# Splitting a W2 tile over TensorE's column groups by feature instead of by rank, and turning it on VectorE

## The chip, the cores and the metric

The kernel runs on one core of one Trainium2 chip. The metric is the time of one execution on the device, in microseconds (us). A core has five engines that run their own instruction queues in order and wait for each other by semaphores: TensorE (PE, with its weight loads shown as PEld), VectorE (DVE), ScalarE (ACT), GpSimd (POOL) and SyncE (SP), which here only issues DMAs.

## The reference

All data are fp32. `x` is 16 x 512 x 512 (batch, time, features), `cond` 16 x 512.

```python
# layer 0: low-rank adapters that are computed from cond
c = layernorm(cond) * ln_gamma + ln_beta
h = gelu(c @ W1 + bias1)                       # 16 x 512
w = h @ W2 + bias2                             # 16 x 16384, W2 is 512 x 16384 (32 MB)
a1, b1, a2, b2 = [t.reshape(16, 512, 8) for t in split(w, 4)]      # rank 8
mid = gelu(x @ base_down + (x @ a2) @ b2.T)    # per batch row
out = mid @ base_up.T + (mid @ b1) @ a1.T
x = x + (x + out)
# layer 1: a recurrence over time
xW = x @ Wx + b
h_t = tanh(xW_t + h_(t-1) @ Wh)
x = x + h
```

## The kernel before

Features lie on the 128 partitions, in KT = 4 blocks; time runs through the kernel in 16 chunks of 32 steps. After a setup stage the recurrence takes step after step, and the dense products of the next chunk are placed between its steps, slot by slot.

The setup stage computes the adapters. `h` is laid out as `h_rep`: 32 columns, (group, repeat, batch). W2 is cut into 16 tiles of 1024 columns = 128 features x 8 ranks, in the order a2, b2, b1, a1 (`W2_TILES`, numbers n = 0 to 15); a tile comes in two halves of K, so there are 32 halves i = 2n, 2n+1 of 1 MB each. SyncE loads them into a ring of four buffers (`load`, L443); the load into a used buffer waits on `row_mm`, until the half that was in it has been multiplied. `down`, `up` and `Wx` go through the same ring; `Wx` is ring entry 30, between halves 27 and 28, and its buffer is then used by the last half, 31, whose load waits on `w_split`: until `Wx` has been split into a rounded high part (ScalarE, L604) and a remainder (VectorE, L679).

The steps of the stage are numbered i = 0 to 40 and written out on each engine's queue:

- TensorE, step i: `row(i)` (L935) multiplies half i: for each of its HK = 2 K blocks and each of 4 column groups one fp32 matmul, which is two instructions in the trace, so 16 a half. `h_rep` is the stationary operand (32 columns), W2 the moving one. Column group j writes PSUM partitions 32j to 32j+31 with the 256 columns that the view `"p (k m j)"` gives it: every fourth column of the tile, which are ranks j and j+4 of all 128 features. `row(2n)` waits until the PSUM bank that it reuses has been emptied (`row_done`, tile n-2).
- ScalarE, step 2n+1: `row_copy(n)` (L548) copies the 128 x 256 result from PSUM to `wrow` in SBUF.
- TensorE, step 2n+2: `spread(n)` (L920) turns `wrow` with two 128 x 128 transposes into the PSUM tile `rec`, which then has features on the partitions and (rank, group, repeat, batch) along the columns.
- VectorE, step 2n+3: `factor(n)` (L739) adds bias2 and writes `fac`.
- For b2 and a1 (tiles 4 to 7 and 12 to 15) TensorE turns `fac` back with two transposes in step 2n+3 (`turn`, L906).
- ScalarE `factor_high` (L541) and VectorE `split_factor` (L745) split the result into a rounded high part and a remainder, in steps 2n+3 and 2n+4.

Between these, each engine does the work of chunk 0 that is due in the step (`dense_slot(0, i)`): the dense matmuls L957 and the low-rank ones L946 and L960, copies and splits, so that the first recurrence step can start when the stage ends. PSUM and the buffers are double-buffered by n % 2.

Of the kernel before, what the change touches and what calls it, by code (L numbers as in the profile page):

```python
# [5 lines left out]
P = 128  # L6
# [8 lines left out]
RANK = 8  # L15
# [9 lines left out]
REPS = 2  # L25
# [12 lines left out]
BANK_ROW = 4  # L38
# [4 lines left out]
COLG = 4  # L43
BANK_IDLE = 0
SQ = 32
# [78 lines left out]
def build(nc: bass.Bass, x, cond, down, up, gamma, beta, w1, bias1, w2, bias2, wx, wh, b, y):  # L124
    B, T, D = x.shape
    KT = D // P
# [8 lines left out]
    HALVES = 2 * 4 * KT  # L135
# [4 lines left out]
    with ExitStack() as ctx:  # L140
        def sb(name, shape, dt=F32):
            return ctx.enter_context(nc.sbuf_tensor(name, shape, dt))
# [4 lines left out]
        def sem(name):  # L147
            return ctx.enter_context(nc.semaphore(name))
# [51 lines left out]

        w1_f = work[:, RING, :].rearrange("p (k n) -> p k n", k=KT)

        wrow = sb("wrow", [P, 2, WCOLS])
        cn = gel[0:B]
        vecs = hf[0:4 * KT].rearrange("p s k b -> p (s k b)")[:, 0:P]
        ln = sb("ln", [B, 8])
# [48 lines left out]
        up_hi = sem("up_hi")  # L255
        row_mm = sem("row_mm")
        row_done = sem("row_done")
        fac_mm = sem("fac_mm")
        fac_done = sem("fac_done")
        fac_tr = sem("fac_tr")  # L260
        fac_split = sem("fac_split")
# [44 lines left out]
        def w2_entry(i):  # L306

            e = W2_ENTRY + i
            return e if e < WX_ENTRY else e + 1
# [18 lines left out]
        def need(eng, s, n):  # L328

            if not isinstance(n, int) or n > 0:  # L330
                eng.wait_ge(s, n)
# [175 lines left out]
        def _(act):  # L507
# [32 lines left out]
                    act.wait_ge(fac_tr, turned_count(n))  # L540
                nc.scalar.copy(dst[:, HI], src).then_inc(fac_hi, 1)  # L541

            def row_copy(n):

                act.wait_ge(row_mm, 2 * n + 2)
                if n >= 2:
                    act.wait_ge(fac_mm, n - 1)
                nc.scalar.copy(wrow[:, n % 2, :], bulk[:, BANK_ROW + n % 2, 0:WCOLS]).then_inc(row_done, 1)  # L548

            def place(n, f):  # L550

                c, t = n // TC, n % TC
# [36 lines left out]
                                         bias=bs[:, m:m + 1], scale=fwd).then_inc(xw_done, 1)  # L589

            for i in range(STREAM + 1):
                if i % 2 and i < HALVES:
                    row_copy(i // 2)
                for n in range(LAST + 1):
                    if i == 2 * n + 3:
                        factor_high(n)
                if i == UP3_AT:
                    up_high(KT - 1)
                if i == WH_HI_AT:
                    act.wait_ge(scl_done, 1)  # L600
                    nc.scalar.activation(wh_s[:, 0], wh_f, ACT.Identity, scale=w_scale).then_inc(wh_hi, 1)
                if i == WX_HI_AT:
                    arrived(act, WX_ENTRY)
                    nc.scalar.copy(wx_s[:, HI], wx_f).then_inc(w_hi, 1)  # L604
                dense_slot(0, i)
                for r in NEXT_ACT.get(i, ()):
                    dense_slot(1, r)
# [25 lines left out]
        def _(dve):  # L633
# [83 lines left out]
            nc.vector.tensor_scalar(z0s[:], Z0, fwd, None, ALU.mult).then_inc(z0_done, 1)  # L717
            split_up(KT - 1)

            def factor(n):  # L720

                q, dt = W2_TILES[n]
                f = fac[:, n % 2]
                dve.wait_ge(fac_mm, n + 1)
                if n == 0:
                    dve.wait_ge(small_in, 64)
                if n >= 2:
                    dve.wait_ge(fac_split, n - 1)
                sums = rec[:, n % 2, 0:RANK * REPS * B]
                bias = bias2T[:, q, dt:dt + 1, :]  # L730
                if q in (1, 2):
                    out = f[:, :, 0]
                    sums = sums.rearrange("p (r g e b) -> p g e b r", r=RANK, g=GROUPS, e=REPS)[:, :, 0]
                    bias = bias.rearrange("p (o a) r -> p o a r", o=1).broadcast_to([P, GROUPS, GB, RANK])
                else:
                    out = f.rearrange("p g e b r -> p (g e b) r")
                    sums = sums.rearrange("p (r c) -> p c r", r=RANK)
                    bias = bias.broadcast_to([P, REPS * B, RANK])
                nc.vector.tensor_tensor(out, sums, bias, ALU.add).then_inc(fac_done, 1)  # L739
# [61 lines left out]

            for i in range(STREAM + 1):
                for n in range(LAST + 1):
                    if i == 2 * n + 3:
                        factor(n)
                for n in range(LAST + 1):
                    if i == 2 * n + (3 if W2_TILES[n][0] in (1, 2) else 4):
                        split_factor(n)
                if i == WH_LO_AT:
                    dve.wait_ge(wh_hi, 1)  # L810
                    nc.vector.scalar_tensor_tensor(out=wh_s[:, 1], in0=wh_f, scalar=w_scale, in1=wh_s[:, 0],
                                                   op0=ALU.mult, op1=ALU.subtract).then_inc(wh_split, 1)
                if i == WX_LO_AT:
                    split_weight(1, wx_f, wx_s)
                dense_slot(0, i)
                for r in NEXT_DVE.get(i, ()):
                    dense_slot(1, r)
# [36 lines left out]
        def _(pe):  # L854
# [47 lines left out]
            def turn(n):  # L902

                pe.wait_ge(fac_done, n + 1)
                for g in range(GROUPS):
                    last = nc.tensor.transpose(turned(n)[:, g * P:(g + 1) * P],  # L906
                                               fac[:, n % 2, g].rearrange("p e b r -> p (e b r)"), ident[:])
                last.then_inc(fac_tr, 1)

            def spread(n):  # L910


                pe.wait_ge(row_done, n + 1)
                if n == 1:
                    pe.wait_ge(z0_done, 1)
                if n >= 2:
                    pe.wait_ge(fac_split, n - 1)
                wv = wrow[:, n % 2, :].rearrange("p (d s) -> p d s", s=RANK // COLG)
                for r in range(RANK // COLG):
                    last = nc.tensor.transpose(rec[:, n % 2, r * P:(r + 1) * P], wv[:, :, r], ident[:])  # L920
                last.then_inc(fac_mm, 1)

            def row(i):


                n, half = i // 2, i % 2
                if i == 0:
                    pe.wait_ge(hT_done, 1)
                if n >= 2 and half == 0:
                    pe.wait_ge(row_done, n - 1)  # L930
                arrived(pe, w2_entry(i))
                raw = work[:, w2_entry(i) % RING, :].rearrange("p (k m j) -> p k m j", k=HK, j=COLG)
                for k in range(HK):
                    for j in range(COLG):
                        last = nc.tensor.matmul(bulk[j * SQ:(j + 1) * SQ, BANK_ROW + n % 2, 0:WCOLS],  # L935
                                                h_rep[:, half * HK + k].rearrange("p g e b -> p (g e b)"), raw[:, k, :, j],
                                                start=(half == k == 0), stop=(half == 1 and k == HK - 1),
                                                skip_group_check=True)
                last.then_inc(row_mm, 1)
# [94 lines left out]
            for i in range(STREAM + 1):  # L1034
                if i < HALVES:
                    row(i)
                if i % 2 == 0 and 0 <= i // 2 - 1 <= LAST:
                    spread(i // 2 - 1)
                if i % 2 and 0 <= i // 2 - 1 <= LAST and W2_TILES[i // 2 - 1][0] in (0, 3):
                    turn(i // 2 - 1)  # L1040
                if i == UP3_AT:
# [62 lines left out]
```

## Time and profile before

| | |
|---|---|
| time of the kernel before, median of 3 runs | 1273.57 us (1273.09 to 1273.87) |
| the profiled execution's own time | 1275.12 us |
| its span, first to last instruction | 1273.4 us |
| mean granted TensorE clock | 0.990 |
| TensorE busy | 1234.6 us (97%) |
| VectorE busy | 906.0 us (71%) |
| ScalarE busy | 632.8 us (50%) |
| GpSimd busy | 280.3 us (22%) |
| HBM read and written | 55.68 MB, 16.78 MB |

The profile shows one execution. The busy times are averages over a short setup stage and a long recurrence, which have different limits; which of them bears on the change has to be read from the stage in which it lies, with the chain of waits and the tables by window. Busy times of TensorE are modelled at the ends of its matmuls, so the distance from one start to the next says more than a duration.

### The profile page before, as it was taken

The numbers are of one execution on the slowest core, as the hardware profiler recorded it, in microseconds if no ns is written. First come the engines' busy times: TensorE is split into PE (matmuls) and PEld (weight loads), VectorE is DVE, ScalarE is ACT, GpSimd is POOL, SyncE is SP. The second block draws the span as 40 slices with busy tenths as digits, with TensorE's granted clock in tenths as the row PEclk, the third lists the DMA queues.
The fourth block names the chain that finished last, engine by engine and source line by source line (L and its number), as shares of the span: only waits on it lengthen the run. The fifth ranks groups of instructions, "written<-read, shape, count | busy, mean of one in ns | idle before, by whom it ended". The sixth has DMA issues, their size and how long they took to land.

```text
span 1273.4 us, 49421 instructions
## 1 busy us (share of the span) xinstructions
PE 1234.6 (97%) x20440; PEld 991.3 (78%) x20440; DVE 906.0 (71%) x3659; ACT 632.8 (50%) x2449; POOL 280.3 (22%) x523
## 2 busy tenths in 40 slices
PE   6899899999999999999999999999999999999996
PEld 5344688888888888888888888888888888888764
DVE  4322467777878787877778787878787787877564
ACT  2221355555555555555554555555555555555442
POOL 0000022222222222222222222222222222222211
PEclk9899999999999999999999999999999999999998
DMA  7998501212112131212111221312121212101022
GB/s 233 393 316 284 100 11 28 36 25 37 29 27 44 19 52 19 44 28 37 32 29 27 36 36 21 50 20 45 27 42 29 35 22 35 18 10 28 2 36 35
DMA packets 284081, 75.66 MB, mean 59 GB/s; under 512 B 273073, under 2 KB 273089, under 8 KB 283857
## 3 DMA queue, kind: packets, MB, share of 16 engines
q1 hardware_dynamic: 277488, 71.89, 24.7%
q8 instruction: 162, 2.65, 0.9%
q10 hardware_dynamic: 6368, 0.60, 0.4%
q14 instruction: 63, 0.51, 0.2%
HBM read 55.68 MB, written 16.78 MB: 57 GB/s over the span
## 4 chain that ended last, share of the span: by engine, by line
PE 91%; DMA 2%; ACT 2%; DVE 2%; SPq 1%; issue 1%; ACTq 0%; DVEq 0%; POOLq 0%; POOL 0%
PE bulk L957 44%; PE rec L973 32%; PE bulk L946 5%; PE bulk L960 5%; PE bulk L935 3%; DMA work<-in_L_cond_W_dram 2%; ACT hf L617 1%; SPq L448 1%; DVE z L830 1%; ACT rec L555 1%; PE bulk L887 1%; DMA hf<-in_L_cond_b_dram 0%; PE rec L920 0%; DVE work L799 0%; PE rec L906 0%
## 5 line engine op out<-in xcount | busy, mean ns | idle before, releaser
L973 PEld LDWEIGHTS rec<-hs,wh_s 128*128 128x128 f16 x16352 | 442.6, 96 | 129.0 <-DVE hs L838 125.4
L617 ACT ACTIVATE hf<-z,scl 128x32 f32<-128x32 f32 x1024 | 273.9, 315 | 485.3 <-DVE z L830 480.7
L973 PE MATMUL rec<-hs,wh_s 128*128 128x32 f16 x16352 | 493.3, 177 | 7.0 <-ACT rec L555 7.0
L503 POOL TENSOR_TENSOR work<-work,hf 128x64 f32<-128x64 f32 x512 | 278.8, 545 | 983.0 <-DVE hs L838 983.0
L830 DVE TENSOR_REDUCE z<-rec 128x32 f32<-128x96 f32 x1022 | 231.3, 256 | 113.5 <-PE rec L973 100.2
L835 DVE TENSOR_SCALAR hs<-hf 128x32 f16<-128x32 f32 x1024 | 181.7, 177 | 105.8 <-ACT hf L617 105.8
L957 PE MATMUL bulk<-act_x,down_s 128*128 128x512 f32 x768 | 219.9, 410 | 2.8 <-ACT work L588 2.8
L838 DVE SCALAR_TENSOR_TENSOR hs<-hf,hs 128x32 f16<-128x32 f32 x1024 | 197.4, 193 | 35.3
L957 PE MATMUL bulk<-mid_s,up_s 128*128 128x512 f32 x768 | 217.2, 406 | 0.0
L957 PE MATMUL bulk<-act_s,wx_s 128*128 128x512 f32 x768 | 206.2, 405 | 0.0
L555 ACT ACTIVATE rec<-work 128x32 f32<-128x32 f32 x1022 | 183.7, 210 | 0.0
L957 PEld LDWEIGHTS bulk<-act_s,wx_s 128*128 128x128 f32 x768 | 134.8, 188 | 22.0
L957 PEld LDWEIGHTS bulk<-act_x,down_s 128*128 128x128 f32 x768 | 133.2, 191 | 23.5 <-ACT work L588 3.0
L957 PEld LDWEIGHTS bulk<-mid_s,up_s 128*128 128x128 f32 x768 | 131.6, 188 | 18.3 <-issue 0.9
L935 PE MATMUL bulk<-work,h_rep 128*32 128x256 f32 x512 | 63.9, 628 | 12.6 <-DMA work<-in_L_cond_W_dram 12.6
L588 ACT ACTIVATE work<-bulk,bs,scl 128x512 f32<-128x512 f32 x64 | 47.8, 776 | 17.9 <-PE bulk L957 17.4
L935 PEld LDWEIGHTS bulk<-work,h_rep 128*32 128x32 f32 x512 | 14.8, 119 | 41.0 <-issue 25.4
L786 DVE SCALAR_TENSOR_TENSOR work<-work,bulk 128x512 f32<-128x512 f32 x64 | 43.6, 681 | 3.8 <-PE bulk L960 2.3
L960 PE MATMUL bulk<-rank_s,a_s 128*128 128x256 f32 x256 | 45.9, 292 | 0.0
L960 PE MATMUL bulk<-rank_s,b_s 128*128 128x256 f32 x256 | 45.6, 292 | 0.0
L799 DVE STREAM_TRANSPOSE work<-work 128x512 f32<-128x512 f32 x64 | 44.7, 702 | 0.5 <-POOL work L503 0.5
L782 DVE TENSOR_TENSOR mid_s<-gel,mid_s 128x512 fp32r<-128x512 f32 x64 | 43.8, 684 | 1.7 <-ACT mid_s L578 1.6
(107 smaller groups left out, 760.2 us busy)
## 6 DMA issues: line engine op xcount, KB each, us to landing
work<-in_L_cond_W_dram SPq DMA_DIRECT2D x33, 1024.0 KB, 7.3
work<-in_x_dram SPq DMA_DIRECT2D x256, 64.0 KB, 3.5
out_dram<-work SPq DMA_DIRECT2D x248, 64.0 KB, 2.3
work<-in_L_cond_base_up_dram SPq DMA_DIRECT2D x1, 1024.0 KB, 7.8
work<-in_L_cond_base_down_dram SPq DMA_DIRECT2D x1, 1024.0 KB, 10.5
work<-in_L_cond_Wh_dram SPq DMA_DIRECT2D x1, 1024.0 KB, 13.0
work<-in_L_cond_Wx_dram SPq DMA_DIRECT2D x1, 1024.0 KB, 7.5
out_dram<-work ACTq DMA_DIRECT2D x8, 64.0 KB, 3.2
```

The source lines that it names most:

```text
L503: nc.gpsimd.tensor_tensor(xs, xs, hf[:, t % 4], ALU.add).then_inc(sum_done, 1)
L555: nc.scalar.activation(R[f][:, :, PARTS, :], xw[:, c % 2].rearrange("p k (b t) -> p k b t", t=TC)[:, f * HT:(f + 1) * HT, :, t], ACT.Copy) ...
L588: nc.scalar.activation(xw[:, n % 2, m], bulk[:, BANK_XW[m], :], ACT.Identity, bias=bs[:, m:m + 1], scale=fwd).then_inc(xw_done, 1)
L617: nc.scalar.activation(hf[:, t % 4, half], z[:, half], ACT.Tanh, scale=inv).then_inc(tanh_done, 1)
L830: nc.vector.tensor_reduce(z[:, half], R[f].rearrange("p m j b -> p m b j"), AX.X, ALU.add).then_inc(z_done, 1)
L835: nc.vector.tensor_scalar(hs[:, half, 0, :], hf[:, t % 4, half], H_SCALE, None, ALU.mult).then_inc(hi_done, 1)
L838: nc.vector.scalar_tensor_tensor(out=hs[:, half, 1, :], in0=hf[:, t % 4, half], scalar=H_SCALE, in1=hs[:, half, 0, :], op0=ALU.mult, op1=A ...
L935: last = nc.tensor.matmul(bulk[j * SQ:(j + 1) * SQ, BANK_ROW + n % 2, 0:WCOLS], h_rep[:, half * HK + k].rearrange("p g e b -> p (g e b)"), ...
L946: last = nc.tensor.matmul(bulk[:, out_bank, g * GC:(g + 1) * GC], fac_s[:, k, g, :], src[:, a, k, g * GC:(g + 1) * GC], start=(k == g == a ...
L957: mm = nc.tensor.matmul(bulk[:, banks[m], :], w_s[:, w, k, m * P:(m + 1) * P], src[:, a, k, :], start=(i in starts), stop=(i in ends), ski ...
L960: mm = nc.tensor.matmul(bulk[:, banks[m], k * GC:(k + 1) * GC], rank_f[:, -1 - p, k, m * P:(m + 1) * P], rank_s[:, k * GC:(k + 1) * GC], s ...
L973: last = nc.tensor.matmul(R[fo][:, m, 0:PARTS, :], wh_s[:, q, k, n * P:(n + 1) * P], hs[:, k, :, :], start=(m == k == q == 0), stop=(k == ...
```

## The change

Three things change together. The column groups of the W2 product take contiguous parts of the tile: group j gets features 32j to 32j+31 with all 8 ranks, which are 256 adjacent columns, where it had ranks j and j+4 of all 128 features, every fourth column. The result of a tile, still 128 partitions x 256 columns in PSUM, then consists of 32 x 32 blocks that only have to be transposed each in place, and VectorE does that straight from PSUM into the SBUF tile `wturn` (`row_turn`, step 2n+2). ScalarE's `row_copy` and TensorE's `spread` go, and with them the semaphore `fac_mm`; `factor` reads `wturn` instead of `rec`. Waits that `spread` carried for the reuse of `rec` move into `turn`.

```diff
-        wrow = sb("wrow", [P, 2, WCOLS])
+        wturn = sb("wturn", [P, 2, RANK * SQ])
...
-            def row_copy(n):
-
-                act.wait_ge(row_mm, 2 * n + 2)
-                if n >= 2:
-                    act.wait_ge(fac_mm, n - 1)
-                nc.scalar.copy(wrow[:, n % 2, :], bulk[:, BANK_ROW + n % 2, 0:WCOLS]).then_inc(row_done, 1)
...
-                if i % 2 and i < HALVES:
-                    row_copy(i // 2)
...
+            def row_turn(n):
+
+                dve.wait_ge(row_mm, 2 * n + 2)
+                need(dve, fac_done, n - 1)
+                nc.vector.transpose(wturn[:, n % 2].rearrange("p (r c) -> p r c", r=RANK),
+                                    bulk[:, BANK_ROW + n % 2, 0:WCOLS].rearrange(
+                                        "p (d r) -> p r d", r=RANK)).then_inc(row_done, 1)
+
             def factor(n):
 
                 q, dt = W2_TILES[n]
                 f = fac[:, n % 2]
-                dve.wait_ge(fac_mm, n + 1)
+                dve.wait_ge(row_done, n + 1)
...
-                sums = rec[:, n % 2, 0:RANK * REPS * B]
+                sums = wturn[:, n % 2]
...
                 for n in range(LAST + 1):
+                    if i == 2 * n + 2:
+                        row_turn(n)
                     if i == 2 * n + 3:
                         factor(n)
...
             def turn(n):
 
                 pe.wait_ge(fac_done, n + 1)
+                pe.wait_ge(fac_split, n - 1)
+                if n == KT:
+                    pe.wait_ge(up_split, KT)
+                if n == KT + 1:
+                    pe.wait_ge(z0_done, 1)
...
-            def spread(n):
-
-
-                pe.wait_ge(row_done, n + 1)
-                if n == 1:
-                    pe.wait_ge(z0_done, 1)
-                if n >= 2:
-                    pe.wait_ge(fac_split, n - 1)
-                wv = wrow[:, n % 2, :].rearrange("p (d s) -> p d s", s=RANK // COLG)
-                for r in range(RANK // COLG):
-                    last = nc.tensor.transpose(rec[:, n % 2, r * P:(r + 1) * P], wv[:, :, r], ident[:])
-                last.then_inc(fac_mm, 1)
...
-                raw = work[:, w2_entry(i) % RING, :].rearrange("p (k m j) -> p k m j", k=HK, j=COLG)
+                raw = work[:, w2_entry(i) % RING, :].rearrange("p (k j m) -> p k j m", k=HK, j=COLG)
...
-                                                h_rep[:, half * HK + k].rearrange("p g e b -> p (g e b)"), raw[:, k, :, j],
+                                                h_rep[:, half * HK + k].rearrange("p g e b -> p (g e b)"), raw[:, k, j, :],
...
-                if i % 2 == 0 and 0 <= i // 2 - 1 <= LAST:
-                    spread(i // 2 - 1)
```

## Rows read from the trace of the kernel before

**Rows 1.** The page, part 1: busy us (share of span) and instructions.

```profile
PE 1234.6 (97%) x20440; PEld 991.3 (78%) x20440; DVE 906.0 (71%) x3659; ACT 632.8 (50%) x2449; POOL 280.3 (22%) x523
```

**Rows 2.** The chain of waits, 15 to 165 us: start us, us, what.

```profile
30.94 10.89 DMA work<-in_L_cond_W_dram
...
41.97 2.04 PE bulk L935 x16
...
44.02 9.48 DMA work<-in_L_cond_W_dram
...
53.64 2.00 PE bulk L935 x16
55.63 0.43 PE rec L920 x2
...
121.69 1.92 PE bulk L935 x16
...
124.51 2.21 DVE wx_s L679
...
126.74 5.37 DMA work<-in_L_cond_W_dram
...
132.16 2.04 PE bulk L935 x16
...
143.48 8.19 PE bulk L957 x36
151.66 1.92 PE bulk L946 x16
...
156.39 3.78 PE bulk L957 x8
```

**Rows 3.** Waits of SyncE's queue, 0 to 160 us: us, times, longest.

```profile
SPq L443 <- PE bulk L935: 77.9, 26, 6.4
```

**Rows 4.** Windows: length, busy of each engine, PEclk, DMA share, GB/s.

```profile
40.00:60.00 20.00, 18.61 (x133) 6.72 (x126) 9.91 (x20) 6.49 (x13) 0.00 (x0) 1.00 1.03 409
60.00:120.00 60.00, 60.00 (x422) 27.54 (x421) 13.33 (x29) 10.59 (x28) 0.00 (x0) 1.00 0.93 325
```

**Rows 5.** Windows over half 2 and half 11, same columns.

```profile
36.78:38.73 1.95, 1.95 (x16) 0.55 (x17) 0.00 (x0) 0.00 (x0) 0.00 (x0) 0.50 1.03 424
65.15:67.07 1.92, 1.92 (x17) 0.45 (x16) 0.00 (x0) 0.00 (x0) 0.00 (x0) 1.00 0.94 367
```

**Rows 6.** Weight loads by source line, 60 to 130 us: ns min/median/max.

```profile
L920 PEld LDWEIGHTS rec<-ident,wrow x22: 195/206/219, 62.8 to 129.7; 128*128 128x128 f32 x22
...
L906 PEld LDWEIGHTS rec<-ident,fac x12: 139/140/143, 67.1 to 127.4; 128*128 128x128 f32 x12
```

**Rows 7.** Instruction fetches, 40 to 60 and 60 to 120 us: packets, MB.

```profile
q8 instruction: 1, 0.02, 0.3%
q14 instruction: 1, 0.01, 0.1%
...
q8 instruction: 4, 0.07, 0.5%
```

**Rows 8.** Timelines of ScalarE, VectorE, TensorE: start us, us, what, idle before.

```profile
120.66 1.91 ACT L604 CAST wx_s<-work 128x2048 fp32r<-128x2048 f32 x1
...
40.46 0.68 DVE L692 TENSOR_TENSOR up_s<-bulk,up_s 128x512 fp32r<-128x512 f32 x1
...
136.62 0.44 PE L906 MATMUL rec<-ident,fac 128*128 128x128 f32 x2 [1.00 <-DVE fac L739]
```

**Rows 9.** Groups by line to 180 us (mean ns); L752 by source line.

```profile
L548 ACT COPY wrow<-bulk 128x256 f32<-128x256 f32 x16 | 5.9, 372 | 74.7 <-PE bulk L935 74.7
...
L739 DVE TENSOR_TENSOR fac<-rec,bias2T 128x256 f32<-128x256 f32 x8 | 3.4, 424 | 13.3 <-PE rec L920 13.3
...
L739 DVE TENSOR_TENSOR fac<-rec,bias2T 128x128 f32<-128x128 f32 x8 | 2.3, 288 | 10.5 <-PE rec L920 10.5
...
L752 DVE STREAM_TRANSPOSE work<-work x64: 666/703/707, 47.3 to 1119.5; 128x512 f32<-128x512 f32 x64
```

More of the change, by code:

```diff
@@ L257, in build @@
         row_done = sem("row_done")
-        fac_mm = sem("fac_mm")
         fac_done = sem("fac_done")
```

## The prediction, made blind

> **What bounds the kernel now.** I read the page first: TensorE is busy for 97% of the span [rows 1], so the question is where in the span the change sits. The chain of waits answers it. From about 160 us on it is the recurrence, which the change does not touch. The changed code lives in the first 135 us, the W2 stage, and that stage has three parts. Until 53.64 us each half (16 matmul instructions of L935) starts when its load lands: half 4 starts at 41.97 on a load landed at 41.83, and the load of half 8 is issued at 44.02 and lands 9.48 us later, at 53.50 [rows 2]. From 53.64 to 121.69 us, halves 8 to 28, the chain never leaves TensorE: 68.05 us for 20 halves. SyncE confirms who is slow there: it waits 77.9 us in 26 waits for L935 to free a ring slot before it may issue the next load [rows 3]. The stage moves 325 GB/s in 60 to 120 us, against 409 GB/s in 40 to 60 us, where loads set the pace [rows 4]. Last, from 124.51 us, VectorE's rounding remainder of Wx (L679, 2.21 us) releases the last load, which takes 5.37 us, and half 31 starts only at 132.16 us [rows 2].
>
> **TensorE loses the turns.** Each of the 16 tiles had two transposes (L920), 0.43 us on the chain [rows 2]. The turns of tiles 3 to 12 stand between 53.64 and 121.69 us: 10 x 0.43 = 4.3 us. The earlier three hide behind the loads. Tile 13's turn goes from the path to the last load, see below; the last two stand behind waits too.
>
> **The product changes its operand.** The number of instructions, columns and bytes stays; the 256 moving columns of each were 16 bytes apart and become adjacent. Does the distance cost anything? Half 2 ran while the granted clock was 0.50 (1.2 GHz) and took 1.95 us; half 11 ran at 1.00 (2.4 GHz) and took 1.92 us [rows 5]. The dense matmuls beside it do follow the clock: 36 take 8.19 us at the high level (0.23 each), 8 take 3.78 us at the low one (0.47 each) [rows 2]. So at 2.4 GHz the array is not what limits a half; its array work is at most half of 1.95, 0.98 us, and the rest must be feeding it. Another spaced read points to the cause: weight loads of L920, elements 8 bytes apart, take 206 ns in the median, those of L906, adjacent, 140 ns, same shape and clock [rows 6]. I therefore take the spacing as the limit and 1.05 us for a half after the change (0.98 plus a little for the ends, which don't scale). The bounds are 0.98 and the unchanged 1.92.
>
> The Trainium skill has a rule for this: "Advanced Engine Details and Errata", section "SBUF Cachelines", says that SBUF is read in lines of 16 bytes, that two hits per line are needed for full speed, and that a new line at each access is penalised. The old spacing gives one hit per line, adjacent columns four; by that rule the half gets faster, and the sum is the one above. That two hits are enough does not agree with the 206 against 140 ns of L920, where two elements share a line.
>
> **TensorE's new sum.** The 68.05 us hold 20 x 1.92 = 38.4 of halves, 4.3 of turns, and so 25.3 of other work. After: 20 x 1.05 + 25.3 = 46.3 us. If nothing else came in, half 28 would start 21.7 us earlier. It can't: the loads can't follow.
>
> **The loads become the limit.** A load is 1024 KiB = 1.049 MB; at 409 GB/s [rows 4] that is 2.56 us. The load of half 8 lands at 53.50; Wx is the 20th after it. With a ring of four, a load is issued when the half four earlier is done, now about 1 us after that half's own load, so the queue always holds about three. So 20 x 2.56 = 51.2. The trace also has instruction fetches on the same engines: in 40 to 60 us one of 16 KB and one of 8 KB [rows 7], and over the four loads from 41.83 to 53.50 the last landing came 11.67 - 4 x 2.56 = 1.4 us late. In 60 to 120 us there are four of 16 KB [rows 7]; the 47 us after that which the loads need have some 50 of the 64 KB. At the same price that is 2.9 us; I take 3.0, with bounds 0 (it lands on idle engines) and 6. Wx lands at 53.50 + 51.2 + 3.0 = 107.7 us.
>
> **The last load.** It waits for both halves of the Wx split. ScalarE's cast takes 1.91 us [rows 8], VectorE's remainder 2.21 to 2.28; with 0.1 of semaphores, 107.7 + 4.3 = 112.0 us. VectorE is free for it: row_turn(13) needs only half 27, done some 3 us before, where factor(13) used to wait for a turn queued behind half 28 (121.69 + 1.92 + 0.43). Alone the load would land at 112.0 + 5.37 = 117.4, but the loads of halves 28 to 30 are ahead, landing by 107.7 + 3 x 2.56 = 115.4, so 118.0. TensorE meanwhile does halves 28 to 30 and what follows each (6 dense matmuls, 1.4, two transposes, 0.4, and 4 low-rank matmuls, 0.5), and stands ready at about 117.1. Half 31 runs 118.1 to 119.2 us; before, 132.16 + 1.92 = 134.1. **The stage ends 14.9 us earlier.**
>
> **What VectorE and ScalarE pay.** ScalarE loses 16 copies of 372 ns [rows 9], in idle time: nothing. VectorE gains 16 transposes. None of this shape is in the trace. The transpose of 512 columns takes 703 ns, as other operations of 512 columns do, and the bias add of 256 columns, which reads PSUM with gaps, 424 ns [rows 9]. Between 0.29 (the same add of 128 columns) and 0.70 I take the nearest row's 0.43 us, 6.9 in all. It lies in idle time: VectorE is busy 13.3 of 60 us in 60 to 120 us [rows 4], 0.74 for each of the 18 halves there, and with 0.22 more it stays under 1 us in a period of 2.7. Queued behind row_turn(n) on VectorE are split_factor and the rounding work of the same slots; for row_turn(n) itself half 2n+4 waits, two tiles on, over 4 us later. The tightest place is the first: VectorE gets to row_turn(0) only after L692, started 40.46 and 0.68 long [rows 8], so it ends near 41.6; half 4 has to have it, and its load lands at 41.83. That is 0.2 us of cover; if it is gone, TensorE waits some tenths in a part where the loads set the pace. The bias add reads SBUF instead of PSUM: no change to within 0.05 us. The waits moved into turn(n) are for work two tiles back: nothing.
>
> **The tail.** After half 31 TensorE waits 1.00 us for factor(15) [rows 8], which VectorE does only after work that ScalarE and the turn of tile 14 feed; that chain starts at the end of half 31 and stays, with row_turn(15) inside it. Everything from there, including the low-clock stretch around 156.39 us, moves forward as it is.
>
> **Sum.** 14.9 us off. The profiled execution took 1275.12 us with a span of 1273.4, 1.5 above the median of the runs, and would be 1260.2; the median 1273.57 becomes 1258.7 us.
>
> **Rivals.** *A, the forecast: halves get fast and the loads set the pace.* From the bounds: no late fetches 1256.3, twice as many 1261.8; a half of 1.4 us costs 1 to 2 more. *B, the half does not get faster* because the four groups share one feed of moving columns, whatever their spacing. For it: 1024 columns at the dense rate of 0.2275 us per 512 are 0.455 us, close to 1.92 / 4. Against it: the same duration at half the clock, where an array-bound half would need nearly 3.8 us. Then TensorE stays the limit until half 28, 4.3 us sooner at 117.4. Half 27 ends at 115.6; turn(12) and its two splits, then the cast (1.91) and the remainder end near 120.5 instead of 126.7. The last load lands 6.1 us earlier: 1267.5. *C, slower: the clock falls.* TensorE will now wait for loads in most halves. If waits of up to 1 us brought the low level and it held through the stage, halves would take 1.95 [rows 5] and the 25.3 us become 50.6: 39.0 + 50.6 = 89.6 instead of 68.05, and the 16.5 us of work from 137.06 (after the turn of tile 15) to 153.58 us [rows 2, 8] double too: 1273.6 + 21.6 + 16.5 = 1311.7. A half at the low level costs 0.9, its share of the other work 1.3, less 0.4 of waiting that it covers, so from about 8 such halves on the gain is gone. Against it: between 40 and 60 us TensorE has such gaps already (18.61 busy of 20) and the clock was 1.00 [rows 4]. *D, VectorE late:* with 5.4 us per tile and 1.5 of other work, a turn sets the pace from 3.9 us on and costs the whole gain from about 5.2. What other operations of this size take [rows 9] speaks against it. *E, the low level near 156 us does not come:* 8 matmuls in 3.78 us [rows 2] would take 1.8, 1.9 less: 1256.8; a second such stretch would give 1260.6.
>
> **Chances.** A 0.62, B 0.22, E or another short stretch of clock 0.05, something between A and B (halves of 1.6 us, loads in bursts) 0.05, C 0.03, D and a queue that I misjudge 0.03. Likeliest: 1258.7; A's own range is 1255.5 to 1262. The range that also takes in B is 1255 to 1268. A measurement of this kernel can tell about 0.2%, 2.5 us, from no change. Faster 0.93, same 0.03, slower 0.04.
>
> **What the new profile would show.** Right: a half at clock 1.00 near 1.05 us; in 60 to 105 us a rate near 400 GB/s and TensorE waiting for W2 loads; half 31 near 118 us; turns (row_turn) of 0.43 us on VectorE; the rest shifted by one amount. Wrong: halves still 1.92 us and no load waits (B); PEclk below 1.00 between 55 and 135 us (C); row_turn as a releaser of L935 (D).

## The result, and the profile after

| | before | after |
|---|---|---|
| median of 4 runs each, same comparison | 1273.33 us (1272.0 to 1273.87) | 1258.45 us (1257.64 to 1261.45) |
| ratio, 95% interval | | 0.9886 (0.9874 to 0.9898) |
| the profiled execution's own time | 1275.12 us | 1258.02 us |
| its span | 1273.4 us | 1256.3 us |
| mean granted TensorE clock | 0.990 | 0.985 |

The change saves 14.9 us by the medians and 17.1 us between the two profiled executions. Before's profiled one was 1.8 us above the median here, after's 0.4 below, so the pair overstates the gain by 2.2 us.

In the code of after the W2 product is L927 (L935 before), VectorE's turn L714, `factor` L737, `split_factor` L743, TensorE's turn-back L911, the dense matmuls L949, the low-rank ones L938 and L952, the cast of Wx L594, its remainder L669, SyncE's loads L442.

Part 1 of the page of after, against [rows 1]: TensorE has 28.4 us less to do, VectorE 8.0 more.

```profile
PE 1206.2 (96%) x20408; PEld 988.1 (79%) x20408; DVE 914.0 (73%) x3675; ACT 627.6 (50%) x2433; POOL 280.2 (22%) x523
```

Windows of after (columns as in [rows 4]): two stretches of the stage, then half 4 and half 8 alone, then the dense work behind half 31.

```profile
40.00:60.00 20.00, 15.99 (x145) 7.73 (x138) 12.04 (x23) 4.64 (x9) 0.00 (x0) 0.80 1.03 410
60.00:105.00 45.00, 38.29 (x381) 23.11 (x380) 16.82 (x36) 7.99 (x18) 0.00 (x0) 1.00 1.03 407
41.43:43.40 1.97, 1.93 (x16) 0.66 (x16) 1.97 (x2) 0.00 (x0) 0.00 (x0) 0.50 1.04 416
52.97:54.05 1.08, 1.08 (x17) 0.55 (x17) 0.00 (x0) 0.00 (x0) 0.00 (x0) 1.00 1.03 410
119.90:126.90 7.00, 7.00 (x26) 5.59 (x26) 3.46 (x6) 2.25 (x4) 0.00 (x0) 0.78 0.57 89
```

Between 60 and 120 us TensorE was busy all the time before, and the loads ran at 325 GB/s [rows 4]. Now, in 60 to 105 us, it is busy 38.29 of 45 us and the loads run at 407 GB/s, close to the 409 of 40 to 60 us before. A half takes 1.08 us at a granted clock of 1.00 (2.4 GHz) and 1.97 at 0.50 (1.2 GHz). Before it took 1.92 and 1.95 [rows 5], so it has begun to follow the clock.

The granted clock was 0.80 in 40 to 60 us, where it was 1.00 before [rows 4]: the low stretch at the start of the stage now lasts until about 48 us, where it ended at about 40 before. It cost nothing that shows, since the loads set the pace there: in the run w1 below half 4 took 1.10 us instead of 1.97, and the load of half 8 landed at 52.63 us, against 52.84 here.

The chain of waits of after (start us, us, what), against [rows 2]:

```profile
43.41 9.43 DMA work<-in_L_cond_W_dram
...
52.97 1.07 PE bulk L927 x16
...
56.70 8.94 DMA work<-in_L_cond_W_dram
...
82.27 9.04 DMA work<-in_L_cond_W_dram
...
103.71 1.00 PE bulk L927 x16
104.71 0.38 PE rec L911 x2
...
105.47 0.38 ACT a_s L540
...
105.88 0.44 DVE a_s L743
...
106.34 0.69 DVE rank_s L776
...
107.06 0.62 DVE fac L737
107.68 2.30 DVE wx_s L669
...
110.00 5.16 DMA work<-in_L_cond_W_dram
...
115.20 1.07 PE bulk L927 x16
...
119.88 7.01 PE bulk L949 x24
...
140.28 3.58 PE bulk L949 x8
143.86 0.81 PE rec L965 x32
144.67 1.48 PE bulk L949 x6
```

The stretch that never left TensorE now runs through DMA pieces of about 9 us: each is a load that was issued when a ring slot came free and then queued behind the others. The end of the stage is built as before (remainder of Wx, last load, half 31), but starts earlier: half 31 ends at 116.27 instead of 134.20 us, 17.9 us sooner. The recurrence then starts at 143.86 instead of 160.17 us, 16.3 sooner: 1.54 us of the 1.6 lost on the way are in the 24 dense matmuls, which took 7.01 us at a mean clock of 0.78 and took 5.47 before. The 6 dense matmuls after the first recurrence step go the other way, 1.48 us where they took 2.26.

Groups by line to 165 us, and a wait of SyncE's queue (us, times, longest), against [rows 9] and [rows 3]:

```profile
L927 PE MATMUL bulk<-work,h_rep 128*32 128x256 f32 x512 | 39.2, 429 | 24.0 <-DMA work<-in_L_cond_W_dram 23.8
...
L714 DVE STREAM_TRANSPOSE wturn<-bulk 128x256 f32<-128x256 f32 x16 | 7.1, 445 | 29.4 <-PE bulk L927 29.4
...
L737 DVE TENSOR_TENSOR fac<-wturn,bias2T 128x256 f32<-128x256 f32 x8 | 4.8, 600 | 0.1
...
SPq L442 <- PE bulk L927: 63.6, 26, 6.7
```

The product is 39.2 us of TensorE where it was 32 halves of 1.92, and TensorE's idle time before it, 24.0 us, is now nearly all spent waiting for W2 loads. SyncE still waits 63.6 us for a half to free its buffer, but three to four loads are under way meanwhile, and the DMA engines are busy throughout (share 1.03, rate 407 GB/s). VectorE's turn takes 445 ns. The bias add has the same shape as before, but takes 600 ns instead of 424: its source is now in SBUF with 128 bytes between the elements that it reads one after the other.

### The profile page after: what moved, and what is told of

Read it like the earlier page. It is cut to its first block, busy times and chain, and to the rows that moved or that the text cites. A ratio compares the mean times of both kernels' runs of the same rounds, so it can differ in the third digit from the quotient of the medians.

```text
span 1256.3 us, 49350 instructions
## 1 busy us (share of the span) xinstructions
PE 1206.2 (96%) x20408; PEld 988.1 (79%) x20408; DVE 914.0 (73%) x3675; ACT 627.6 (50%) x2433; POOL 280.2 (22%) x523
## 4 chain that ended last, share of the span: by engine, by line
PE 89%; DMA 5%; ACT 2%; DVE 2%; SPq 1%; issue 1%; ACTq 0%; DVEq 0%; POOLq 0%; POOL 0%
PE bulk L949 44%; PE rec L965 32%; PE bulk L938 5%; PE bulk L952 5%; DMA work<-in_L_cond_W_dram 4%; ACT hf L607 1%; PE bulk L927 1%; SPq L447 1%; DVE z L830 1%; ACT rec L547 1%; PE bulk L887 1%; DMA hf<-in_L_cond_b_dram 0%; DVE work L797 0%; DVE wx_s L669 0%; ACT work L580 0%
## 5 line engine op out<-in xcount | busy, mean ns | idle before, releaser
L949 PE MATMUL bulk<-act_x,down_s 128*128 128x512 f32 x768 | 219.0, 408 | 2.8 <-ACT work L580 2.8
L949 PE MATMUL bulk<-mid_s,up_s 128*128 128x512 f32 x768 | 217.6, 406 | 0.0
L949 PE MATMUL bulk<-act_s,wx_s 128*128 128x512 f32 x768 | 207.4, 407 | 0.0
L949 PEld LDWEIGHTS bulk<-act_s,wx_s 128*128 128x128 f32 x768 | 135.5, 189 | 22.2
L949 PEld LDWEIGHTS bulk<-act_x,down_s 128*128 128x128 f32 x768 | 132.5, 190 | 22.8 <-ACT work L580 3.0
L949 PEld LDWEIGHTS bulk<-mid_s,up_s 128*128 128x128 f32 x768 | 132.0, 189 | 19.3 <-issue 1.6
L927 PE MATMUL bulk<-work,h_rep 128*32 128x256 f32 x512 | 39.2, 429 | 24.0 <-DMA work<-in_L_cond_W_dram 23.8
L580 ACT ACTIVATE work<-bulk,bs,scl 128x512 f32<-128x512 f32 x64 | 47.8, 776 | 17.9 <-PE bulk L949 17.4
L927 PEld LDWEIGHTS bulk<-work,h_rep 128*32 128x32 f32 x512 | 15.1, 118 | 43.4 <-DMA work<-in_L_cond_W_dram 24.4
L952 PE MATMUL bulk<-rank_s,a_s 128*128 128x256 f32 x256 | 46.0, 293 | 0.0
L952 PE MATMUL bulk<-rank_s,b_s 128*128 128x256 f32 x256 | 45.6, 292 | 0.0
```

Source lines behind the costliest of these rows:

```text
L580: nc.scalar.activation(xw[:, n % 2, m], bulk[:, BANK_XW[m], :], ACT.Identity, bias=bs[:, m:m + 1], scale=fwd).then_inc(xw_done, 1)
L949: mm = nc.tensor.matmul(bulk[:, banks[m], :], w_s[:, w, k, m * P:(m + 1) * P], src[:, a, k, :], start=(i in starts), stop=(i in ends), ski ...
L952: mm = nc.tensor.matmul(bulk[:, banks[m], k * GC:(k + 1) * GC], rank_f[:, -1 - p, k, m * P:(m + 1) * P], rank_s[:, k * GC:(k + 1) * GC], s ...
```

## The experiments

**The spacing alone, and the turn alone.** `e1_adjacent_only` gives the kernel before adjacent columns and leaves ScalarE's copies and TensorE's turns as they were, so that its features come out in another order. `e2_spaced_turned` gives the changed kernel every fourth column again.

```diff
# e1, on the kernel before
-                raw = work[...].rearrange("p (k m j) -> p k m j", k=HK, j=COLG)
+                raw = work[...].rearrange("p (k j m) -> p k j m", k=HK, j=COLG)
...
-                    raw[:, k, :, j],
+                    raw[:, k, j, :],
```

> The kernel before with one edit: each column group multiplies 256 adjacent columns. ScalarE's copy and TensorE's turns (L920) stay as they were, so they now turn other columns into a place and the output isn't the reference's; instructions, bytes and waits are those of before. Theory 1 (the spacing of the moving columns limited a half, after the change the loads set the pace): halves take 1.05 us at the high clock, TensorE's sum from half 8 to 28 is 46.3 + 4.3 = 50.6 us, just under the 51 to 54 us of the loads, half 28 starts near 107 us; the remainder of Wx waits for the turn behind half 28 again, so half 31 starts near 116.5 us: 1 to 2 us slower than the changed kernel, 1259.5 to 1260.5 us, ratio to before about 0.989 to 0.990. Rival (the gain comes from moving the turns off TensorE and from the earlier last load): halves stay at 1.92 us and the time stays within 2 us of before.

> The changed kernel with one edit: the column groups take every fourth column again, as before; VectorE turns the result as after the change, so the values land in other places and the output isn't the reference's. Theory 1: halves take 1.92 us, TensorE is the limit again from half 8 to 28, 4.3 us shorter than before, the last load is issued near 120.5 us: 6 us less than before, 1267.5 us, ratio 0.995 to 0.996. Rival (the turns are the gain): about the time of the changed kernel, 1258 us.

Measured: e1 1259.64 us (1258.71 to 1260.03), ratio 0.9891 (0.9875 to 0.9908); e2 1266.52 us (1266.41 to 1270.14), ratio 0.9955 (0.994 to 0.997). A window and the chain of e1, then the same window, the product's group and the chain of e2:

```profile
60.00:105.00 45.00, 41.27 (x400) 25.82 (x398) 13.01 (x28) 10.57 (x26) 0.00 (x0) 1.00 1.03 407
...
108.97 2.21 DVE wx_s L679
...
111.20 5.19 DMA work<-in_L_cond_W_dram
...
116.44 1.07 PE bulk L935 x16
```

```profile
60.00:105.00 45.00, 45.00 (x330) 19.73 (x326) 14.11 (x30) 7.42 (x17) 0.00 (x0) 1.00 0.96 338
...
L927 PE MATMUL bulk<-work,h_rep 128*32 128x256 f32 x512 | 63.1, 629 | 12.0 <-DMA work<-in_L_cond_W_dram 12.0
...
120.41 5.29 DMA work<-in_L_cond_W_dram
...
125.74 1.99 PE bulk L927 x16
```

Adjacent columns alone make the half 1.07 us and hand the stage to the loads; the copies and turns that e1 still does cost it 1.24 us at half 31 (116.44 against 115.20). The medians differ by 1.2 us too, which their intervals do not separate. The turn alone leaves TensorE busy without a gap, at 338 GB/s, and brings the issue of the last load 6.3 us forward (120.41 against 126.74), where rival B had 6.1 for its landing. The two parts gain 13.3 and 6.5 us by the medians against 1272.98 of that comparison, more in sum than the 14.9 of both, because with fast halves the loads set the pace and time taken from TensorE is hidden.

**How much adjacency is needed.** `e3_pairs` gives each column group every second column of one half of a K block, 8 bytes apart, so that two of the columns that it reads lie in every 16 bytes. The features come out in another order.

```diff
-                raw = work[...].rearrange("p (k j m) -> p k j m", k=HK, j=COLG)
+                raw = work[...].rearrange("p (k h m s) -> p k h m s", k=HK, h=2, s=2)
...
-                    raw[:, k, j, :],
+                    raw[:, k, j // 2, :, j % 2],
```

> The changed kernel, but the moving columns of a group are 8 bytes apart (every second column of one half of the tile), so that two of them share a 16-byte line; the output isn't the reference's. If any gap halves the feeding, as the weight loads of L920 suggest: halves of 1.92 us and the time of the run with every fourth column, 1267.5 us. If two columns per 16-byte line are enough, as the Trainium skill (Advanced Engine Details and Errata, SBUF Cachelines) says: halves of 1.05 us and 1258 us. In between (some 1.4 us a half) if the first and second access of a line cost differently.

Measured: 1256.57 us in one run. The product's group and a half on the chain of e3:

```profile
L927 PE MATMUL bulk<-work,h_rep 128*32 128x256 f32 x512 | 40.4, 438 | 23.9 <-DMA work<-in_L_cond_W_dram 23.7
...
105.44 1.04 PE bulk L927 x16
```

Columns 8 bytes apart run nearly like adjacent ones, 438 against 429 ns, and those 16 bytes apart take 629.

One thing changes together with the distance: in e2 all four groups read from the same 16 bytes, in e3 two of them do, and with adjacent columns each group has them for itself. So these runs don't tell whether a half is slow because each group finds one column in 16 bytes, or because four groups read the same 16 bytes at once; no run here separates the two.

**Are the loads the new limit?** `e4_half_loads` loads only the first K block of each half, 512 KB, and multiplies it twice; the other half of W2 is left out. The work of every engine stays.

```diff
-                    src, kt = w2_v[:, i % 2 * HK:(i % 2 + 1) * HK, c0:c0 + W2C], HK
+                    src, kt = w2_v[:, i % 2 * HK:i % 2 * HK + 1, c0:c0 + W2C], HK
...
-                    raw[:, k, j, :],
+                    raw[:, 0, j, :],
```

> The changed kernel, but each of the 32 W2 loads brings only the first of its two K blocks (512 KB), and both blocks' matmuls use it; the other half of W2 is left out of the computation. Instruction counts and waits stay. Theory 1 (loads set the pace after the change): the pace goes to TensorE, whose work from half 8 to 28 is 46.3 us, and the runs of waits before half 8 shrink too: half 8 near 44 us, half 28 near 90 us, stage end near 100 instead of 116 us, 1242 us (1238 to 1248). Rival (another chain, over VectorE's turns or ScalarE, sets the pace in the changed kernel): less than 4 us faster than the changed kernel, 1254 us or more.

Measured: 1242.94 us in one run. A window and the chain of e4:

```profile
55.00:90.00 35.00, 34.96 (x360) 22.25 (x359) 16.06 (x35) 7.98 (x18) 0.00 (x0) 1.00 0.78 260
...
97.60 3.84 DMA work<-in_L_cond_W_dram
...
101.48 1.07 PE bulk L927 x16
```

With half the bytes TensorE fills the stage again (34.96 of 35 us) and half 31 starts 13.7 us earlier. So half of the bytes of W2 are worth 13.7 us to the changed kernel. Of these, 5.4 us come ahead of half 8, which starts at 47.53 instead of 52.97. From half 8 to half 28 TensorE needs 46.4 us (to 93.97) instead of 54.0 (to 106.99). The prediction's sum for TensorE alone over this stretch was 46.3. So the loads hold back the W2 stream behind half 8 by some 7.5 us.

**Is VectorE near the path?** `e5_turn_twice` does each turn a second time, into a spare tile. `l1_turn_layout` lets the turn write the ranks innermost, so that the bias add reads adjacent elements and the turn writes with gaps.

```diff
# e5
+                need(dve, extra, n)
+                nc.vector.transpose(spare[:].rearrange("p (r c) -> p r c", r=RANK), ...).then_inc(extra, 1)
# l1
-                nc.vector.transpose(wturn[:, n % 2].rearrange("p (r c) -> p r c", r=RANK),
+                nc.vector.transpose(wturn[:, n % 2].rearrange("p (c r) -> p r c", r=RANK),
...
-                    sums = sums.rearrange("p (r c) -> p c r", r=RANK)
+                    sums = sums.rearrange("p (c r) -> p c r", r=RANK)
```

> The changed kernel with each turn done twice on VectorE: an additional transpose of the same 256 columns into a spare tile stands ahead of the real one, with a wait for the one before, so 16 x 0.45 = 7.2 us of VectorE work more. Theory 1 (VectorE is hidden except on the path to the last load and between half 31 and factor(15)): at most 0.45 us at each of these two places, 1258.5 to 1259.5 us, and the loads land as before. Rival (VectorE in order is what TensorE or the loads wait for in every tile): 4 to 7 us slower, 1262 us or more.

> The changed kernel, but row_turn writes wturn with the rank innermost (elements 32 bytes apart within a 32 x 32 block), so that the bias add reads 256 adjacent elements instead of elements 128 bytes apart. The bias add of 256 columns took 600 ns from SBUF after the change, 424 ns from PSUM before. Theory 1 (its widely spaced SBUF read costs the difference): 424 ns again, the turn stays near 445 ns, and 0.2 us each comes off the path to the last load and off the tail, 1258.0 us, which one look can't tell from 1258.4. Rival (SBUF as a source costs it, or the spaced write moves the cost into the turn): the sum of turn and add stays at 1.05 us.

Measured: 1257.45 and 1260.3 us, one run each. Groups of e5 (its second turn), then of l1:

```profile
L720 DVE STREAM_TRANSPOSE wturn<-bulk 128x256 f32<-128x256 f32 x16 | 6.5, 406 | 0.0
```

```profile
L714 DVE STREAM_TRANSPOSE wturn<-bulk 128x256 f32<-128x256 f32 x16 | 10.7, 668 | 30.8 <-PE bulk L927 30.8
...
L737 DVE TENSOR_TENSOR fac<-wturn,bias2T 128x256 f32<-128x256 f32 x8 | 3.3, 418 | 0.1
```

16 turns more, with which VectorE's turns take 6.5 us longer in all, move nothing beyond the spread of the changed kernel's runs. In l1 the add falls from 600 to 418 ns and the turn rises from 445 to 668: 1086 against 1045 ns for the pair. The gap costs about as much on whichever side it is.

**Can the last load start earlier?** `w1_wx_earlier` moves Wx four entries up in the ring and its split four steps.

```diff
-WX_HI_AT, WX_LO_AT = 28, 29
+WX_HI_AT, WX_LO_AT = 24, 25
...
-        WX_ENTRY = HALVES + 2 - 4
+        WX_ENTRY = HALVES + 2 - 8
```

> The changed kernel with Wx four ring entries earlier (26 instead of 30) and its two split operations in steps 24 and 25 instead of 28 and 29, so that the load that waits for the split is that of half 27 and not the last. In the changed kernel the load of half 30 lands at 111.84, that of half 31, issued at 110.00 after the split, only at 115.16 us. Theory 1 (there the issue and not the stream decides): loads land 2.56 us apart to the end, half 31's at 114.4 to 114.6 us, unless the split is late in the new place too; 0.6 to 0.8 us less in this stage. Rival (the split only moves the stall: half 27's load is issued late and the stream tears there): half 31's load at 115.2 us or later.

Measured: 1256.45 us in one run. The chain of w1:

```profile
107.16 8.32 DMA work<-in_L_cond_W_dram
...
115.53 1.07 PE bulk L927 x16
...
120.14 5.46 PE bulk L949 x24
```

The wait for the split is gone, and the last load lands at 115.48 us all the same, where it landed at 115.16. It now stands in the queue behind the others, as the rival for this run had it. The lower time is not from there; in this execution the 24 dense matmuls took 5.46 us instead of 7.01.

**Can the stream of loads start earlier?** SyncE's queue also issues the 16 loads of `x` for chunk 0 ahead of half 2's. Before them it waits until W1, which shares a ring buffer, has been used. `x4_x_on_scalar` issues them from ScalarE. `x6_w1_own` gives W1 its own buffer and drops the wait; `x7_w1_own_wx_early` is x6 with w1's edit. `x8_x_split` is x6 with half of the `x` loads four entries later, and `x9_x_last` is the changed kernel with all of them four entries later.

```diff
# x4: from SyncE to ScalarE, after up_high(KT - 1)
-                if e == RING - 1:
-                    sp.wait_ge(hT_mm, 1)
-                    for k in range(KT):
-                        load_x(0, k)
...
+                    for k in range(KT):
+                        for q in range(P // SQ):
+                            act.dma_start(xn[...], rows(x, 0, k)[q]).then_inc(x_in[k], 16)
# x6
-        w1_f = work[:, RING, :].rearrange("p (k n) -> p k n", k=KT)
+        w1_f = sb("w1_own", [P, KT, 512])[:]
...
-                    sp.wait_ge(hT_mm, 1)
# x8, on x6
-                if e == RING - 1:
-                    for k in range(KT):
+                if e in (RING - 1, 2 * RING - 1):
+                    for k in (0, 1) if e == RING - 1 else (2, 3):
# x9
-                if e == RING - 1:
+                if e == 2 * RING - 1:
```

> The changed kernel, with the 16 loads of x for chunk 0 issued by ScalarE's queue in step 1 instead of by SyncE ahead of the load of half 2; nothing else moves. In the changed kernel SyncE issues them from 16.33 to 28.71 us, and the DMA engines move only 83 to 112 GB/s from 20 to 30 us. Theory 1 (from there on the loads set the pace until the end of the stage, so what starts the stream earlier ends the stage earlier): the loads of halves 2 to 5 are issued near 24 us, the load of half 8 lands near 48.5 to 49.5 instead of 52.84 us, half 31 starts 3.5 to 4.5 us earlier, 1254 us (1253 to 1256), ratio to before 0.984 to 0.986. Rival (the transfers of x, in packets of 128 bytes, take their share of the DMA engines wherever they stand, or x now comes too late for chunk 0): less than 1 us from the changed kernel.

> The changed kernel with W1 in a buffer of its own. Before, W1 lay in the buffer into which x of chunk 0 is loaded, so SyncE waited 9 us for W1's last matmul (16.3 us) before it issued the 16 loads of x, and the load of half 2 stood behind them until 28.76 us. Now x is issued from about 6 us on, while SyncE would wait anyway, and nothing else moves. The run with x on ScalarE's queue brought the load of half 8 down at 46.5 instead of 52.8 us, but then ScalarE sat 30.3 us in its queue of x loads and VectorE's turns waited for it. Theory 1 (a stream that starts earlier ends earlier, if no engine is held): half 2's load is issued near 24 us, half 8's lands at 46 to 48, half 31 starts 4 to 6 us before 115.20 us, time 1252.5 to 1254.5 us, ratio to before 0.984 to 0.986. Rival (some other wait of the first 50 us, such as VectorE's split of Wh or TensorE at 1.2 GHz, holds the halves, so the ring is not freed): less than 2 us gained.

> The run with W1 in its own buffer, and Wx four ring entries earlier as in the run before. There half 31's load landed at 115.48 against 115.16 us in the changed kernel: the stall moved to the load of half 27 and nothing was gained in the stage. Theory 1: the same here, so within 1 us of the run with W1's own buffer alone, 1252 to 1255 us. Rival (with an earlier stream the split is early enough in the new place, and the loads run through to the end): 0.8 to 2 us less than with W1's own buffer alone.

> W1 in a buffer of its own, and the loads of x of chunk 0 in two parts: 8 of the 16 before the load of half 2 and 8 behind the loads of halves 2 to 5. With W1's own buffer alone SyncE's 16 x loads took from 7.51 to 29.07 us, since each waits in its queue behind the megabyte loads, so the load of half 2 still left only at 29 us while the DMA engines were idle for 30 to 50% from 20 to 30 us. Theory (the stream, once it starts, is gapless, and the stage ends as much earlier as it starts): the loads of halves 2 to 5 are issued at 24 to 25 us, half 8's lands 3 to 4 us earlier than 52.84, half 31 starts 2.5 to 4 us before 115.20 us, 1255 us (1254 to 1256). Rival (the second half of x holds SyncE behind the four loads, the ring runs empty behind them, and the time is given back): half 8's load within 1 us of 52.84 us, or later, and 1258 us or more.

> The changed kernel with all 16 loads of x of chunk 0 behind the loads of halves 2 to 5 instead of ahead of half 2's; W1 stays in x's buffer. Theory: the loads of halves 2 to 5 leave near 24 us, those of half 6 and on only when SyncE is through with x, near 38 to 40 us, so the stream tears once, x arrives at 40 to 45 us; half 8's load 0 to 3 us earlier than 52.84 us. Rival (SyncE sits behind the four loads for longer, as ScalarE did for 30.3 us, and x comes too late for chunk 0's first matmuls at 50 us): half 8's load later than 52.84, slower than the changed kernel.

| | median us (range) | ratio to before, 95% | half 8's load lands, us | half 31 starts, us |
|---|---|---|---|---|
| after | 1258.45 (1257.64 to 1261.45) | 0.9886 (0.9874 to 0.9898) | 52.84 | 115.20 |
| x4 | 1269.56 (1267.26 to 1272.59) | 0.9971 (0.996 to 0.9982) | 46.5 | 126.78 |
| x6 | 1258.66 (1256.67 to 1260.52) | 0.9885 (0.987 to 0.9899) | 53.4 | 116.76 |
| x7 | 1257.86 (1256.33 to 1258.54) | 0.9875 (0.9858 to 0.9891) | 53.3 | 116.34 |
| x8 | 1260.51 (1257.21 to 1262.42) | 0.9904 (0.9881 to 0.9927) | 55.0 | 119.31 |
| x9 | 1261.53, one run | | 58.3 | 120.54 |

The issue of the 16 `x` loads on the timelines of ScalarE in x4, and of SyncE in after, x6, x8 and x9 (start us, us over all 16 or 8):

```profile
22.81 30.31 ACTq L587 DMA_DIRECT2D work<-in_x_dram  x16
53.17 2.00 ACT L590 ACTIVATE wh_s<-work,scl 128x2048 f16<-128x2048 f32 x1 [29.78 <-issue]
```

```profile
16.33 12.38 SPq L447 DMA_DIRECT2D work<-in_x_dram  x16
```

```profile
7.51 21.52 SPq L447 DMA_DIRECT2D work<-in_x_dram  x16
```

```profile
27.61 13.46 SPq L447 DMA_DIRECT2D work<-in_x_dram  x8
41.12 19.43 SPq L442 DMA_DIRECT2D work<-in_L_cond_W_dram  x8
```

```profile
25.38 19.10 SPq L447 DMA_DIRECT2D work<-in_x_dram  x16
```

These issues hold the queue that makes them, and in these runs for longer when more 1 MB loads are under way. In x6 they begin 8.8 us earlier and take 9.1 us more, so the W2 loads behind them start no sooner: both theories for x6 missed that, though the rival had the size right (less than 2 us). In x4 the W2 stream does start early, but ScalarE stands for 30.3 us, its casts come late, VectorE behind it, and half 6 waits for the turn of tile 1 until 58.36 us. The waits of x4 (us, times, longest):

```profile
PE bulk L926 <- DVE wturn L713: 18.2, 1, 18.2
```

This is rival D's wait, brought about from another engine; the granted clock was 0.50 from 30 to 60 us in this run, so not all of its 11 us need be the wait. x8 and x9 put the held queue into the W2 stream itself: half 31 starts 4.1 and 5.3 us later, and the time is 2.1 and 3.1 us longer, which for x8 its interval doesn't separate from the changed kernel and for x9 rests on one run. No version is better than the changed kernel by more than these measurements tell; x7 is within its range.

## Why the prediction came out right

The forecast was case A, 1258.7 us; measured 1258.45. The mechanism, fast halves first and then loads that set the pace, is shown by e1, e2 and e4. The terms of the sum were less exact than the total.

- **The half.** Predicted 1.05 us at 2.4 GHz and limited by the clock; measured 1.00 to 1.11, and 1.97 at 1.2 GHz. e2 gives the 1.92 back. Rival B, one feed shared by the groups, is refuted. In before and after alike the matmuls of the four groups start within 0.03 us of each other, but the next four follow after 0.45 us before (65.15 and 65.59) and 0.22 after (55.80 and 56.02), where B's shared feed needs 0.455. One piece of evidence was no evidence: L920's weight loads, 206 against 140 ns [rows 6], were read as a cost of elements 8 bytes apart. e3 shows that moving columns 8 bytes apart cost next to nothing. The Trainium skill's rule ("Advanced Engine Details and Errata", "SBUF Cachelines": two hits on a 16-byte line are enough) agrees with 438 against 629 ns for these columns, and not with what the prediction read from L920. What makes L920's loads longer stays open, and so does whether the one hit per line or the sharing of lines by the groups slowed the old halves.
- **The loads.** Half 8's load landed at 52.84 (predicted 53.50), and Wx, 20 loads later, at 104.30 (issued at 95.12, 9.2 us to its landing). That is 51.2 for the loads, as predicted, and 0.3 for late landings, where 3.0 were put down for instruction fetches. This is the largest mis-sized term, 2.7 us. The 1.4 us lag was read wrongly. Between the two landings (41.83 to 53.50 us before) the DMA engines moved 4.77 MB at 409 GB/s, 0.58 MB or 1.4 us more than four loads: they were already at work on the loads behind, and not held up by fetches. Between 52.84 and 104.30 us after the change, they moved 20.99 MB, of which 0.05 were fetches, and the 20 loads are 20.97.
- **The way to the last load.** Predicted 4.3 us from the landing of Wx to the issue; measured 5.7 (104.30 to 110.00). The cast of Wx doesn't start at its landing: ScalarE first does the cast of tile 12, which waits for half 27 and TensorE's turn behind it (103.71 to 105.09), so the cast of Wx begins at 105.74 and ends at 107.64. VectorE, which the prediction had free, was not: the split of tile 12 (L743), that of `rank_s` (L776) and the bias add of tile 13 hold it until 107.68, and the remainder starts there. The prediction had all three engines ready at the landing. The load itself took 5.16 instead of 6.0, since less was ahead of it.
- **Together** half 31 ended at 116.27, 2.9 us before the 119.2 that was predicted: 0.7 from half 8's landing, 2.7 from the fetches, 0.8 from the last load, less 1.4 on the way to it, and 0.1 in the half and rounding. So the stage gained 17.9 us between the profiled executions, not 14.9.
- **VectorE.** 0.43 us for a turn, measured 0.445. It is hidden, as predicted: e5 adds 6.5 us of turns for nothing. The bias add was costed at no change and takes 176 ns more. It is not hidden everywhere: it is on the chain ahead of the remainder of Wx (107.06 to 107.68; the cast of Wx ended 0.04 us before it, so a faster add would gain no more there), and behind half 31, where the add of tile 15 takes 0.59 us instead of 0.43.
- **The clock.** Case E allowed for another short low stretch. Such a stretch came behind half 31 (7.01 for 5.47 us), and cost 1.5 us. The traces of e1, e5, l1 and x4 have it too (6.36 to 6.95 us for these 24 matmuls); those of e2, e3, e4, w1 and x6 to x9 don't (5.46 to 5.49). The long fall of rival C did not come, though TensorE waits for 23.8 us on loads: the granted clock from 60 to 105 us was 1.00. The sign named for C, a clock below 1.00 between 55 and 135 us, did show (0.98 over this stretch), but all of it behind the W2 loads. And the argument against C, that 40 to 60 us already had such waits at a clock of 1.00, did not hold after the change: the clock was 0.80 there. What decides whether the clock falls behind half 31 is not settled; the four executions of the changed kernel differ by 3.8 us, and no run here takes this apart from other causes.
- **The total.** Between the profiled executions the gain is 17.9 us at the end of half 31, 16.1 behind the 24 dense matmuls, 17.2 after the 6 behind the first recurrence step, and 17.1 over the span, where 14.9 was predicted. So the profiled execution of after stood at 1258.02 where 1260.2 was predicted for it. The step from there to the median was 1.5 us down in the prediction and 0.4 up in the runs. The hit to 0.3 us is therefore partly luck; the mechanism alone gave it to about 2 us.
- **A bound.** Without the 3.0 us for fetches every later term moves by 3.0, so the lower figure of case A comes out of its own terms at 1255.7, not 1256.3. The measured time is above both.

## What to carry to other kernels

When a fp32 matmul takes the same time at both levels of the granted clock, look at how its moving operand is read before blaming the array: with two columns of each group in every 16 bytes the half was fast here. When a fix makes the busiest engine faster, find the next limit first (here the loads) and count only the gain up to it. The 16 loads of `x` held the queue that issued them for 12 to 30 us, so where they stood among the large loads mattered more than when they were first allowed to go.

## What the runs showed that was not expected

- The same 16 issues of 64 KB took 12.4 us in after, 21.5 in x6, 19.1 in x9 and 30.3 on ScalarE in x4; the two times 8 of x8 took 15.3 (from 7.47 us) and 13.5 (from 27.61 us, behind four W2 loads). Single ones took 0.34 to 2.62 us in after. Why an issue takes longer was not tried by itself.
- The bias add took 600 ns with 128 bytes between its source elements in SBUF, 418 with adjacent ones there, and 424 from PSUM with gaps [rows 9]. The turn took 445 ns writing whole rows and 668 ns writing with 32 bytes between elements.
- A half with columns 16 bytes apart takes 1.92 us at the high clock level and 1.95 at the low one. At the high level it takes 1.04 to 1.16 us with columns 8 bytes apart, and 1.00 to 1.11 with adjacent ones.
